# Six result buffers, four piece buffers, an exact handover and longer gaps in a six-sweep resampling kernel

## What is computed

```python
center = jnp.einsum('nchw,oc->nohw', feature, w_center)
step = jax.nn.relu(jnp.einsum('nchw,oc->nohw', feature, w_step))
prob = jax.nn.sigmoid(jnp.einsum('nchw,oc->nohw', feature, w_prob))
offset = jnp.transpose(center * step, (0, 2, 3, 1)) * STRIDE
th = jnp.minimum(jnp.round(gh[None] + offset[..., 0]), h - 1)
tw = jnp.minimum(jnp.round(gw[None] + offset[..., 1]), w - 1)
tgt = jnp.mod((th * w + tw).reshape(n, h * w).astype(jnp.int32), h * w)
sample = jax.vmap(lambda idx: grid_flat.at[idx].set(grid_flat))(tgt).reshape(n, h, w, 2)
...
sampled = _grid_sample_bilinear(feature, ngrid)
proped = sampled * prob + feature * (1.0 - prob)
return feature * prob + proped * (1.0 - prob)
```

## Time and profile before

| | us |
|---|---|
| median of 3 runs | 9847.34 |
| lowest, highest | 9839.02, 9898.68 |
| profiled execution | 9910.58 |
| its span, first to last instruction | 9909.0 |
| PE (TensorE matmul) busy | 6574.7 (66%) |
| PEld (weight load, beside PE) busy | 2834.2 (29%) |
| DVE (VectorE) busy | 5644.5 (57%) |
| ACT (ScalarE) busy | 3752.4 (38%) |
| POOL (GpSimd) busy | 4705.3 (47%) |
| mean granted TensorE clock | 0.786 of 2.4 GHz |

### The profile page before, as it was taken

One profiled execution on the slowest core, in us unless ns is written; L12 is line 12 of the kernel. 1 busy time (PEld: TensorE's weight loads), 2 busy tenths in 40 slices (PEclk: granted clock), 3 DMA queues, 4 the chain that ended last, 5 costly groups with the idle time before them and its releaser, 6 DMA issues. The chain is left out here.

```text
span 9909.0 us, 89353 instructions
## 1 busy us (share of the span) xinstructions
PE 6574.7 (66%) x24132; PEld 2834.2 (29%) x24132; DVE 5644.5 (57%) x11270; ACT 3752.4 (38%) x7426; POOL 4705.3 (47%) x8499
## 2 busy tenths in 40 slices
PE   5666455556623677766777578467777674787888
PEld 2222122222211333332333223223333231333333
DVE  2221444336832432226899887328999994466666
ACT  3444333332211333332333023235555263654555
POOL 2333774414433023334577143247887353566665
PEclk7888678777866888886788888776777886888888
DMA  3555444655442455555555146466554264666666
GB/s 141 181 194 205 138 158 161 161 187 176 140 91 92 169 203 196 209 197 174 186 184 205 49 152 221 140 195 179 156 159 141 89 187 112 187 209 206 220 205 201
DMA packets 489217, 1673.51 MB, mean 169 GB/s; under 512 B 119580, under 2 KB 140347, under 8 KB 421396
## 3 DMA queue, kind: packets, MB, share of 16 engines
q1 hardware_dynamic: 214092, 827.29, 27.1%
q10 hardware_dynamic: 210152, 764.05, 20.3%
q0 software_dynamic: 64480, 76.57, 4.4%
HBM read 949.99 MB, written 727.71 MB: 169 GB/s over the span
## 5 line engine op out<-in xcount | busy, mean ns | idle before, releaser
L974 POOL TENSOR_TENSOR arena<-arena 128x32 f32<-128x32 f32 (+8 forms) x3197 | 970.4, 344 | 3445.6 <-PE ps L1161 3442.5
L1161 PE MATMUL ps<-arena,w_conv 128*10 128x400 f32 x3200 | 1572.4, 603 | 1172.3 <-ACT arena L1220 923.1
L1130 PE MATMUL ps<-arena,minus 128*128 128x400 f32 x3200 | 1817.3, 655 | 632.2 <-DVE arena L1026 512.8
L1024 DVE TENSOR_TENSOR ps<-ps,arena 128x400 f32<-128x400 f32 x1600 | 926.4, 579 | 2168.5 <-PE ps L1138 1239.9
L1286 ACT ACTIVATE arena<-ps 128x400 f32<-128x400 f32 x1600 | 800.2, 500 | 2592.7 <-PE ps L1124 755.1
L1220 ACT ACTIVATE arena<-ps 10x400 f32<-10x400 f32 x1600 | 776.4, 492 | 2058.5 <-PE ps L1161 1064.7
L1174 PE MATMUL ps<-ident,arena 128*128 128x128 f32 x5000 | 923.0, 334 | 871.7 <-issue 471.7
L1104 POOL DMA_INDIRECT arena<-table,gidx x800 | 1201.6, 1502 | 602.8 <-PE ps L1147 337.2
L983 POOL TENSOR_TENSOR arena<-arena 128x32 f32<-128x32 f32 (+8 forms) x3197 | 1142.1, 403 | 10.9
L1236 ACT ACTIVATE arena<-ps 128x512 f32<-128x512 f32 (+1 forms) x1400 | 733.3, 550 | 1015.7 <-PE ps L1174 745.1
L1138 PEld LDWEIGHTS ps<-ident,arena 100*128 100x128 f32 x6400 | 825.5, 163 | 880.8 <-issue 741.5
(11 more groups left out here) (205 smaller groups left out, 5844.5 us busy)
## 6 DMA issues: line engine op xcount, KB each, us to landing
arena<-x SPq DMA_DIRECT2D x200, 1600.0 KB, 12.2
arena<-table SPq DMA_DIRECT2D x400, 800.0 KB
table<-arena ACTq DMA_DIRECT2D x400, 512.0 KB
y<-arena ACTq DMA_DIRECT2D x100, 1600.0 KB, 13.8
arena<-y SPq DMA_DIRECT2D x100, 1600.0 KB
out<-arena ACTq DMA_DIRECT2D x100, 1600.0 KB
table<-arena ACTq DMA_DIRECT2D x200, 576.0 KB
conv<-arena ACTq DMA_DIRECT2D x800, 31.2 KB
```

Source lines behind the costliest of these rows:

```text
L974: last = E.tensor_tensor(tmp[:, :, at:at + size], cols[:, :, y + to:end + to:step], cols[:, :, y:end:step], ALU.subtract)
L1024: V.tensor_tensor(d, d, g, ALU.mult).then_inc(s_mix, 1)
L1130: nc.tensor.matmul(ps[:, 4 + r % 2, 0:W], minus[:, :], tile(t)[:, r * W:(r + 1) * W], start=True, stop=False)
L1161: nc.tensor.matmul(ps[0:10, 7 - count % CB, 0:size], w_conv[lt][:, :], tile(t)[:, at:at + size], start=True, stop=True).then_inc(s_conv, 1)
```

## The change

Four edits, and one of names.

- `c_out` has six buffers instead of two. They lie in the same two stretches of SBUF, at partitions 0, 64 and 96 of each (the gates that mixing sweeps load stand at partition 32 there). ScalarE waits for the store of six buffers ago.
- `t_out` has four buffers in sweeps 0 and 1 (`TR`), where the space for table rows is not in use. In sweeps 2 and 3 it keeps two.
- GpSimd's clock after tile t is `(t + behind + 1) * BROWS + 3` instead of `(t + behind + 2) * BROWS + 2`: the slot in which the owner of the tile after t is chosen.
- `blanks(4)` instead of `blanks(2)` ahead of the wait for the halo, in every index generator, and `blanks(2 * BLANKS)`, 12, instead of 6 after the step "src" in those of sweeps 1 and 2.
- Semaphores of loads and stores are made once for all sweeps instead of anew in each, and their counts run on (`counts`, `f0`, `r0`, `y0`, `t0`).

The diff without its hunks that only add `f0`, `r0` or `y0` to a count waited for (`loaded`, `blend_columns`, `hide`, the SP queue and TensorE's waits for rows and gates) and the one of `evacuate_late`:

```diff
--- before.py
+++ after.py
@@ -234,13 +234,15 @@
         rows_at = [used[0], used[0] + STRIPS * HALF * CH2]
         used[0] += 2 * STRIPS * HALF * CH2
         gates_at = [used[0], used[0] + 2 * W]
-        c_out = [part(2 * W, 10) for _ in range(2)]
+        c_out = [again(a, 2 * W, 10, F32, p) for p in (0, 64, 96) for a in gates_at]
+        used[0] += 4 * W
         gate = [part(W) for _ in range(2)]
         sweep_at = used[0]
         T_WORDS = max(TURNED[b - 1][0] + TURNED[b - 1][1] - TURNED[a][0] for a, b in PIECES) * CH2
         t_out = [part(T_WORDS) for _ in range(2)]
         htmp = [part(W) for _ in range(NEARBY)]
         wtmp = [part(BROWS * NFIX).rearrange("p (r n) -> p r n", n=NFIX)]
+        t_out += [again(rows_at[0] + BROWS * NFIX + a * T_WORDS, T_WORDS) for a in range(2)]
         wtmp.append(again(rows_at[0], BROWS * NFIX).rearrange("p (r n) -> p r n", n=NFIX))
         early, late, latened, patch = part(W), part(W), part(W), part(W)
         late_out = part(4 * CH2, LATECOLS)
@@ -292,8 +294,7 @@
         s_const = sem("s_const")
         s_init = sem("s_init")
         s_gath = [sem(f"s_gath{k}") for k in range(DEPTH // GROUP)]
-        s_tst = [sem(f"s_t_st{k}") for k in range(2)]
-        s_cst = [sem(f"s_c_st{k}") for k in range(2)]
+        s_cst = [sem(f"s_c_st{k}") for k in range(len(c_out))]
         s_lst = sem("s_late_st")
         s_xpose = sem("s_xpose")
         s_tevac = sem("s_tevac")
@@ -373,6 +374,12 @@
         s_zact = sem("s_zact")
         s_gatest = sem("s_gatest")
         steps = {"v": 0}
+        s_fld = [sem(f"s_f_ld{a}") for a in range(4)]
+        s_rld = [sem(f"s_rows_ld{a}") for a in range(3)]
+        s_gld = [sem(f"s_gate_ld{a}") for a in range(3)]
+        s_yst = [sem(f"s_y_st{a}") for a in range(4)]
+        s_tst = [sem(f"s_t_st{a}") for a in range(4)]
+        counts = {"f": [0] * 4, "rows": [0] * 3, "y": [0] * 4, "t": [0] * 4}
 
         def indices(u):
 
@@ -494,7 +501,7 @@
                 dve.wait_ge(s_codest, (u + 1) * 16 * 4)
                 yield from piece(V.memset(far, 0.0))
                 yield from piece(V.memset(near, 0.0))
-                yield from blanks(2)
+                yield from blanks(4)
                 dve.wait_ge(s_halo, (u + 1) * 16 * 6)
 
                 loop0 = n[0]
@@ -638,7 +645,7 @@
                     yield from piece(V.tensor_scalar(c0m, c0m, 0.0, None, ALU.is_equal))
                     yield from piece(V.tensor_scalar(c0m, c0m, -1.0, 1.0, ALU.mult, ALU.add))
                     yield from piece(V.scalar_tensor_tensor(c0m, c1m, 1.0, c0m, ALU.add, ALU.mult), "src")
-                    yield from blanks(BLANKS)
+                    yield from blanks(2 * BLANKS)
                 else:
 
                     gidx, gcol, keep = lists[u]
@@ -902,10 +909,15 @@
             GB = 2 if listed else 1
             CB = 1 if mixing else 2
             WB = 1 if mixing else 2
-            s_fld = [sem(f"s_f_ld{k}_{a}") for a in range(FR)]
-            s_rld = [sem(f"s_rows_ld{k}_{a}") for a in range(RR)] if mixing else None
-            s_gld = [sem(f"s_gate_ld{k}_{a}") for a in range(RR)] if mixing else None
-            s_yst = [sem(f"s_y_st{k}_{a}") for a in range(FR)] if mixing else None
+            TR, CR = 2 if mixing else 4, len(c_out)
+            f0, r0, y0, t0 = (list(counts[name]) for name in ("f", "rows", "y", "t"))
+            for t in range(TILES):
+                counts["f"][t % FR] += 1
+                counts["y"][t % FR] += int(mixing)
+            for n in range(2 * TILES):
+                counts["rows"][n % RR] += int(mixing)
+            for n in range(TILES * len(PIECES)):
+                counts["t"][n % TR] += int(tabling)
             if u_idx is not None:
                 vector, scalar, tensor, gpsimd, born = indices(u_idx)
             else:
...
@@ -1092,7 +1104,7 @@
                         for t in range(TILES):
                             if owner[t] == "pool":
                                 blend_columns(pool, nc.gpsimd, t)
-                            clock[0] = (t + behind + 2) * BROWS + 2
+                            clock[0] = (t + behind + 1) * BROWS + 3
                             next(work, None)
                     if listed:
                         for g in range(H // GROUP):
...
@@ -1214,31 +1226,31 @@
                     def evacuate_conv(t, c):
                         n = u_tab * TILES + t
                         count, nth = n * len(CHUNKS) + c, n * PAIRS + c // 2
-                        if c % 2 == 0 and nth >= 2:
-                            act.wait_ge(s_cst[nth % 2], nth // 2 * 16)
+                        if c % 2 == 0 and nth >= CR:
+                            act.wait_ge(s_cst[nth % CR], nth // CR * 16)
                         act.wait_ge(s_conv, count + 1)
-                        nc.scalar.activation(c_out[nth % 2][:, c % 2 * W:(c % 2 + 1) * W], ps[0:10, 7 - count % CB, 0:W],
+                        nc.scalar.activation(c_out[nth % CR][:, c % 2 * W:(c % 2 + 1) * W], ps[0:10, 7 - count % CB, 0:W],
                                              ACT.Copy).then_inc(s_cevac, 1)
                         if c % 2:
                             act.wait_ge(s_cevac, count + 1)
                             at = t * BPX + CHUNKS[c - 1][0]
-                            act.dma_start(convs[u_tab][:, at:at + 2 * W], c_out[nth % 2]).then_inc(s_cst[nth % 2], 16)
+                            act.dma_start(convs[u_tab][:, at:at + 2 * W], c_out[nth % CR]).then_inc(s_cst[nth % CR], 16)
 
                     def evacuate(t, g):
                         n = u_tab * TILES + t
                         count, (j0, size) = turned_before(u_tab, t) + g, TURNED[g]
                         q = [g < b for _, b in PIECES].index(True)
                         a, b = PIECES[q]
-                        nth, at = n * len(PIECES) + q, TURNED[a][0]
-                        if g == a and nth >= 2:
-                            act.wait_ge(s_tst[nth % 2], nth // 2 * 16)
+                        nth, at = t * len(PIECES) + q, TURNED[a][0]
+                        if g == a and nth >= TR:
+                            act.wait_ge(s_tst[nth % TR], (t0[nth % TR] + nth // TR) * 16)
                         act.wait_ge(s_xpose, count + 1)
-                        nc.scalar.activation(t_out[nth % 2][:, (j0 - at) * CH2:(j0 - at + size) * CH2], ps[:, 2 + count % 2, 0:size * PX],
+                        nc.scalar.activation(t_out[nth % TR][:, (j0 - at) * CH2:(j0 - at + size) * CH2], ps[:, 2 + count % 2, 0:size * PX],
                                              ACT.Copy).then_inc(s_tevac, 1)
                         if g == b - 1:
                             act.wait_ge(s_tevac, count + 1)
                             act.dma_start(flat[t][:, at * CH2:(j0 + size) * CH2],
-                                          t_out[nth % 2][:, 0:(j0 + size - at) * CH2]).then_inc(s_tst[nth % 2], 16)
+                                          t_out[nth % TR][:, 0:(j0 + size - at) * CH2]).then_inc(s_tst[nth % TR], 16)
 
                     def evacuate_late(t):
                         n, count = u_tab * TILES + t, turned_before(u_tab, t) + len(TURNED)
...
@@ -1328,14 +1340,14 @@
                     for _ in work:
                         pass
                     if tabling:
-                        n = (u_tab + 1) * TILES
-                        for a in range(2):
-                            act.wait_ge(s_cst[a], n * PAIRS // 2 * 16)
-                            act.wait_ge(s_tst[a], n * len(PIECES) // 2 * 16)
+                        for a in range(CR):
+                            act.wait_ge(s_cst[a], (((u_tab + 1) * TILES * PAIRS - 1 - a) // CR + 1) * 16)
+                        for a in range(TR):
+                            act.wait_ge(s_tst[a], counts["t"][a] * 16)
                         act.wait_ge(s_lst, (u_tab + 1) * len(LATE) * 16)
                     if mixing:
                         for a in range(FR):
-                            act.wait_ge(s_yst[a], (TILES - a + FR - 1) // FR * 16)
+                            act.wait_ge(s_yst[a], counts["y"][a] * 16)
 
         sweep(0, None, 0, None)
         sweep(1, None, 1, 0, pace=0.42, spell=99)
```

More of the change, by code:

```diff
@@ L936, in loaded @@
             def loaded(eng, t):
-                eng.wait_ge(s_fld[t % FR], (t // FR + 1) * 16)
+                eng.wait_ge(s_fld[t % FR], (f0[t % FR] + t // FR + 1) * 16)
             def px(t):
@@ L965, in blend_columns @@
                 if mixing:
-                    eng.wait_ge(s_yst[t % FR], (t // FR + 1) * 16)
+                    eng.wait_ge(s_yst[t % FR], (y0[t % FR] + t // FR + 1) * 16)
                 else:
@@ L1000, in hide @@
                         if m % HALF == 0:
-                            dve.wait_ge(s_rld[j % RR], (j // RR + 1) * 16)
+                            dve.wait_ge(s_rld[j % RR], (r0[j % RR] + j // RR + 1) * 16)
                         s = s_rows[j % RR][:, :, m % HALF, :].rearrange("p q (e c) -> p q e c", e=2)
```

(10 more changed lines are left out.)

## The result

| | before | after |
|---|---|---|
| median (4 runs each) | 9850.69 us | 8674.11 us (8664.86 to 8689.72) |
| ratio, 95% interval | | 0.8799 [0.8766, 0.8832] |
| profiled execution, span | 9910.58, 9909.0 | 8682.99, 8681.4 |
| mean granted clock | 0.786 | 0.824 |

A forecast was written before the change was run, and what follows sets the result against it. No engine was taken as the bound; waits were, for convolution stores and a late GpSimd blend. Terms 815 + 288 + 8 = 1111 us, from the median 9847.34, gave 8736 us; own range 8600 to 8880, 8 in 10 within 8520 to 9040.

The forecast's parts named there:

- Six results: Convolution stores, sweeps 0 to 3: six buffers remove ScalarE's waits on the path; 815 us, extra piece buffers included.
- 25 us at the start of sweep 2 as 0: Sweep 2 before 3088 us: 25.4 us of store waits beside a busy VectorE, 0 to 25, counted as 0.
- 37 us in sweep 3 as 10: Sweep 3, 4480 to 5840 us: 36.8 us of store waits, mostly where VectorE is busy, counted as 10.
- 20 + 8: Sweep 1: 20 us for the wait of 960 to 1040, 8 for 1040 to 1290, where GpSimd has all blends.
- the rival that the clock pays more: After ScalarE's store waits: regained clock saves up to 190 us beyond the sum; time 8550, chance 0.18.
- the 12.1 of the forecast: Sweep 0: the round of 18 us falls to 12.1, set by the ping-pong of TensorE and ScalarE.
- 1.2 was charged: Sweep 2 from 3088 us: 1.2 us a tile taken back for pieces that wait longer with their two buffers.
- The handover: GpSimd's last blend before its pixel moves, sweeps 2 and 3: VectorE's two waits go; 288 us, lower bound 180.
- All S stay within their sweeps: Blanks: S, the slot in which "moved" is issued, shifts by 19 in sweep 1; 0, at most 20 us either way.
- the 8 us of the forecast: Sweep 4: one more group of four rows gathered before the moves, TensorE's wait starts two rows later; 8 us.
- the queue (9090): ScalarE's one store queue: the wait reappears at piece buffers in sweeps 2 and 3; 355 us lost, chance 0.15.
- moved handover (8940): The handover's wait moves to the tile where GpSimd takes over again; 200 of 288 us lost, chance 0.06.

The follow-up runs named there:

- the filler: Kernel before with four more convolution matmuls into an unused bank, ahead of the result that has to wait, in sweep 0 alone: 9844.51 us, ratio 0.9957.

## Why the prediction held, and where its terms did not

The forecast, 8736 us, was the likeliest case, and the time is 8674.11, inside that case's own range. Its gain was 1111; 1177 came.

*Six results.* The mechanism is right: the whole kernel stood still in that wait. The term is undersized. It was 815 with the pieces, 740 without them, and 920 came. Two things made it small. First, waits beside a busy VectorE were counted at nothing or a third: 25 us at the start of sweep 2 as 0, 37 us in sweep 3 as 10. With six results alone the first ten rounds of sweep 2 are 26 us shorter for 25 us of waits, and the first twelve of sweep 3 40 us for 29. "VectorE is busy 981 of 1080 us for the most part" was read from the wrong rounds: only 12 of the 37 us of waits lie in that stretch, and where the other 25 lie VectorE is busy 187 of 280 us. Where the waits stood beside a busy GpSimd the discount was right: the first twelve rounds of sweep 1, charged 20 + 8, are 30 us shorter for 56 us of waits less. The waits that went (905 us), less those for pieces that came (69), are 836 us. Second, the clock. The profiled gain of the four sweeps is 932, 96 more than that. In sweep 0, for instance, the rounds of tiles 12 to 48 get 204 us shorter with six results alone, for 179 us of waits, and the filler shows that there the clock behind the wait is worth something by itself. So the rival that the clock pays more was right in part. The 96 us are less than its 190, and no run shows that all of them are clock. Its ground, that TensorE's speed behind the wait is paid for, held even in sweep 0, where I had counted ScalarE against it.

*Six results and pieces, by sweep.* Sweep 0's round falls from 17.9 to 11.0 us, below the 12.1 of the forecast. Late in sweep 2 it is 23 to 24.4 where 24 to 25 stood. In the last 38 tiles of that sweep the waits for pieces grow from 18.5 to 32.7 us, 0.4 us a tile where 1.2 was charged. In the full change the piece buffers alone are worth 64 us, where the rows showed at most 74.6.

*The handover.* 288 was oversized for the edit alone: 258, within the bounds 180 and 288. "VectorE's blends lengthen the rounds, so I charge nothing" is the step that failed; with the moves beside them the rounds get longer still, and that had to be charged. Rounds 12 to 15 of sweep 2, all with VectorE's blends, take 33 to 36 us with six results and the old handover, and 47 to 49 with the moves beside them. The Trainium skill's rule (SBUF — State Buffer, Who interferes with whom) would have given 251, close to 258. In sweep 2, where most of the price lies, it isn't by what the rule describes: each of VectorE's 11 blends takes 6.6 to 6.7 us, the seven beside the moves like the others. In sweep 1 of the changed kernel 5 of 19 take 7.7 to 10.8 us, with gaps for which the profile shows no releaser; with the new handover alone all 22 take under 7 us, so those are not its price either. What the trace shows in these rounds of sweep 2 is GpSimd's queue taking 26.8% of the DMA engines' time for 5.20 MB (window 2381 to 2574):

```profile
q0 software_dynamic: 3227, 5.20, 26.8%
q1 hardware_dynamic: 3901, 12.81, 19.5%
q10 hardware_dynamic: 2506, 13.07, 16.8%
```

The one store of y whose landing is traced there takes 21.5 us, against 14.5 late in the sweep. In the second profile of the changed kernel it takes 29.2, and TensorE waits 36.7 us for gates in these four rounds, which take 170 us in all instead of 193. That the crowded DMA engines make the rounds longer is likely, not shown: in the first profile most of TensorE's waits there, 55 us against 35 in the same rounds with six results alone, have no releaser in the profile.

*The gaps.* "All S stay within their sweeps, so no work falls behind the last slot: 0, and at most 20 us either way" is wrong for the edit alone: 206 us slower. I had worked out that S moves by 19 in sweep 1 and that S = 226 holds by equality, and did not put the new S into the old clock. In the full change the exact clock covers for it, and there the old gaps made no difference that can be told, as forecast, though not for the reason given: in the faster sweep 1 the moves do run past the first result of its last tile, by 49 us, and lengthen the turn. The same coupling makes the handover worth 375 us in the full change and 258 alone.

*The sum.* The parts alone come to 920 + 258 - 206 = 972 us against 1177 for all, so they don't add. My excess in the handover and my shortfall in the convolution cancelled in part: six results alone gave 180 us more than their term, and the rest of the change on top of them 257 (1177 - 920) where the terms said 371. That the total came within 62 us of the forecast is in that part luck.

*Sweeps 4 and 5.* TensorE's longest wait for gathered rows falls from 86.3 to 78.2 us, the 8 us of the forecast, but the sweep takes 1998 us against 1999. Sweep 5 is 55 us shorter in code that is the same. Windows of sweep 5 (clock, DMA share and GB/s last), the kernel before in the profile of the earlier trace rows, and then the changed kernel as run again (9580.42 us beside it):

```profile
8599.00:9903.00 1304.00, 1084.48 (x4385) 467.01 (x4384) 833.55 (x1591) 645.16 (x1192) 791.08 (x783) 0.84 0.65 205
```

```profile
7330.00:8382.00 1052.00, 970.34 (x4391) 428.44 (x4389) 838.64 (x1594) 654.18 (x1195) 801.45 (x785) 0.95 0.80 255
```

Sweep 5 varies by 250 us between these profiles, so I put none of the 55 down to the change. What makes it vary stays open. The chip by itself isn't shown to: the kernel before took 9580 us in one series and 9867 in another that are both on record as chip 9. Sweeps 0 to 3 have 1171 of the profiled 1227 us.

*The checks named ahead.* Conv waits under 60 us: 14.5. VectorE's longest wait for GpSimd's blend under 15: none in the list. DMA share 0.75 to 0.8 late in sweep 2: 0.81. Mean clock above 0.85: missed, 0.824, since sweeps 4 and 5 with 0.76 and 0.87 hold it down. Waits for pieces, gates and rows stay under 130 us each in this profile; in the second one of the changed kernel those for gates are 209.4 us, and its ratio is 0.8760 all the same. The rivals of the queue (9090) and of the moved handover (8940) did not happen: GpSimd had 133 us to spare before its next tile.

## What to carry to other kernels

When every engine waits for one small store, give it enough buffers for a whole round. Whether another engine's work will take the wait's place is read from the rounds in which the wait stands, not from a longer stretch: with VectorE busy for about three quarters of them (368 of 506 us, 388 of 500) waits came back in full, with GpSimd busy 227 of 250 us about half did. Add what the clock gives back. Before an edit is called neutral because it only shifts slots, put the shifted number into every comparison that reads it, above all one that now holds by equality. Work moved off the path can still lengthen the rounds beside it, here by 13 us each for four rounds: charge them.

## What the runs showed of the hardware

A result's store of 31 KB makes ScalarE wait 4.8 us in sweep 0 with no large store of y in its queue, and 5 us in sweep 2 with y on another queue. In both cases it ends within 2 us after the load of a tile has landed, where that landing is traced. Four extra matmuls in a wait shortened four rounds of sweep 0 from 72 to 65 us, with a granted clock of 1.00 instead of 0.83, and the sweep by 41 us. And the same instructions of sweep 5 took 1304, 1250 and 1052 us in different profiles, at DMA shares of 0.65, 0.68 and 0.80.
